# Narrow attention with outputs scaled by token and packed over two head groups, and layer-norm splits on GpSimd

## The reference

```
q, k, v = heads(h @ Wq), heads(h @ Wk), heads(h @ Wv)          # 16 heads of 16
a   = softmax(q k^T * 0.25)
x   = x + concat_heads(a v) @ W_proj + b_proj                   # 256 x 256
```

## Time and profile before

| | us |
|---|---|
| median of 3 runs (lowest, highest) | 4316.21 (4314.57, 4319.16) |
| profiled execution | 4317.04 |
| its span, first to last instruction | 4315.3 |
| mean granted clock of PE | 0.962 |
| PE, DVE, ACT, POOL busy | 3929.6 (91%), 3012.2 (70%), 2075.9 (48%), 1368.1 (32%) |

### The profile page before, as it was taken

One profiled execution on the slowest core, in us unless ns is written; L12 is line 12 of the kernel. 1 busy time (PEld: TensorE's weight loads), 2 busy tenths in 40 slices (PEclk: granted clock), 3 DMA queues, 4 the chain that ended last, 5 costly groups with the idle time before them and its releaser, 6 DMA issues.

```text
span 4315.3 us, 54472 instructions
## 1 busy us (share of the span) xinstructions
PE 3929.6 (91%) x19916; PEld 2380.8 (55%) x19916; DVE 3012.2 (70%) x4405; ACT 2075.9 (48%) x3756; POOL 1368.1 (32%) x664
## 2 busy tenths in 40 slices
PE   7999989799998888999899968988999999998989
PEld 5343346633334665555555546666555555546778
DVE  5888856788885676777777845445677777774465
ACT  2556655365665533444344436643444444445641
POOL 1100011200001035666566544421444444451120
PEclk7999989999999999999999989998999999998999
DMA  4233240313324133332233223323232333214320
GB/s 132 35 62 47 46 75 22 60 32 50 44 46 76 38 80 74 65 65 56 53 69 69 62 63 82 82 59 78 57 71 64 70 69 69 62 36 115 85 57 20
DMA packets 151979, 269.21 MB, mean 62 GB/s; under 512 B 34090, under 2 KB 67812, under 8 KB 150688
## 3 DMA queue, kind: packets, MB, share of 16 engines
q1 hardware_dynamic: 151712, 265.72, 29.2%
HBM read 105.01 MB, written 29.64 MB: 31 GB/s over the span
## 4 chain that ended last, share of the span: by engine, by line
PE 68%; DVE 16%; issue 4%; SPq 4%; ACT 4%; POOL 2%; DMA 2%; DVEq 0%; POOLq 0%; ACTq 0%
PE PS L1017 30%; PE PS L1196 13%; PE PS L1237 5%; PE PS L1089 4%; PE PS L1093 4%; DVE t L1764 3%; PE PS L1325 3%; PE PS L1247 3%; SPq L2177 2%; DVE t L1758 2%; SPq L2194 1%; DVE PS L1832 1%; DMA t<-t 1%; PE PS L1120 1%; PE PS L1206 1%
## 5 line engine op out<-in xcount | busy, mean ns | idle before, releaser
L1017 PE MATMUL PS<-t 128*128 128x512 f32 (+4 forms) x7896 | 1957.7, 379 | 127.3 <-DVE t L1673 16.5
L1470 ACT ACTIVATE t<-PS 128x512 f32<-128x512 f32 (+2 forms) x1600 | 1165.8, 750 | 989.2 <-PE PS L1017 982.9
L1017 PEld LDWEIGHTS PS<-t 128*128 128x128 f32 (+2 forms) x7896 | 1233.7, 184 | 637.1 <-issue 234.4
L1196 PE MATMUL PS<-t 128*32 128x512 f32 (+2 forms) x4352 | 808.3, 608 | 0.0
L1758 DVE TENSOR_REDUCE t<-PS 128x1 fp32r<-128x1024 f32 x512 | 618.4, 1218 | 232.2 <-PE PS L1089 231.3
L1764 DVE TENSOR_REDUCE t<-PS 128x1 f32<-128x512 f32 x1024 | 647.0, 682 | 65.1 <-PE PS L1093 62.3
L2038 POOL TENSOR_TENSOR t<-t 128x1024 f32<-128x1024 f32 x256 | 620.2, 2423 | 126.8 <-ACT t L1470 101.8
L1089 PE MATMUL PS<-t 128*128 128x512 f32 x1024 | 339.0, 414 | 70.0 <-DVE t L1758 35.6
L1093 PE MATMUL PS<-t 96*128 96x512 bf16 x1024 | 363.5, 392 | 37.6 <-DVE t L1764 21.3
L2034 POOL TENSOR_TENSOR t<-t 128x1024 f32<-128x1024 f32 x64 | 153.8, 2404 | 691.6 <-PE PS L1206 532.9
L1975 POOL TENSOR_TENSOR t<-t 128x2048 f32<-128x2048 f32 x24 | 111.1, 4628 | 819.2 <-DMA t<-in_rows 546.7
(11 more groups left out here) (131 smaller groups left out, 3713.6 us busy)
## 6 DMA issues: line engine op xcount, KB each, us to landing
t<-t SPq DMA_DIRECT2D x640, 128.0 KB, 2.5
t<-scr_n SPq DMA_DIRECT2D x288, 128.0 KB, 6.3
t<-t SPq DMA_DIRECT2D x128, 256.0 KB, 3.8
scr_n<-t SPq DMA_DIRECT2D x72, 256.0 KB, 2.5
t<-t SPq DMA_DIRECT2D x256, 64.0 KB, 2.0
t<-in_L_Wg SPq DMA_DIRECT2D x16, 768.0 KB, 4.6
t<-in_L_W SPq DMA_DIRECT2D x36, 256.0 KB, 3.3
t<-in_L_Wo SPq DMA_DIRECT2D x64, 128.0 KB, 2.4
```

The costliest lines, as they stand in the source:

```text
L1017: ins = e.matmul(out, l, r, start=i == 0, stop=i == len(terms) - 1, tile_position=tp)
L1196: ins = e.matmul(banks[S.ot][wd * j:wd * j + wd, :], u.v[j][kt], P[0:S.pr, j, :], start=kt == 0, stop=kt == S.nkt - 1, tile_position=(0, w ...
L1470: e.activation(dst, src, ACT.Exp, scale=S.L.scale).then_inc(*expd.inc((S.i, i)))
```

## The change

Three edits, in narrow attention and in the layer norms of blocks 0 and 1.

- **Scaling by token.** `sums16` becomes `scale16`: after the same four transposes, DVE takes the reciprocals and at once multiplies the 16 outputs of each head, read from PSUM, by the token's reciprocal, into columns 64 * `ends` of a tile `OT` (`ends` = `g % 2`). `spread16` and the old `norm` are gone.
- **Packing.** Two head groups (units n - 2 and n) fill the 128 columns of an `OT`. Only units with `ends` have a `turn16` (four PE transposes of `OT`, one ACT copy to `ON`) and the two `proj` steps. The projection weights are no longer padded: `S.W` holds 2 slices of 128 rows instead of 4.
- **Splits on GpSimd.** For 8 of the 24 parts (`on_pool`: in blocks 0 and 1 the parts (0,1), (1,0), (1,1) and (2,0), where the pair is sublayer and batch half) the two instructions of `ln_split` are issued on POOL.

The load of an unused constant (`sel`) is dropped, and SBUF pads keep the layout's size. The core of the diff:

```diff
@@ -671,7 +672,9 @@
                 plan.put(now, 0, [("av", S, an, akt)])
                 if akt == S.nkt - 1:
                     plan.put(now + 2e-4, 0, [("fin", S, an)])
-                    todo = [("sums16", S, an), ("spread16", S, an), ("norm", S, an), ("proj", S, an, 0), ("proj", S, an, 1)]
+                    todo = [("scale16", S, an)]
+                    if S.units[an].ends:
+                        todo += [("turn16", S, an), ("proj", S, an, 0), ("proj", S, an, 1)]
                     for at, step in zip(tail, todo):
                         plan.put(now + at, 0, [step])
 
...
@@ -544,7 +544,8 @@
                     u.st = [[[(buf[0:97, 1, j, 128 * kt:128 * kt + 128], buf[0:97, 0, j, q0:q0 + 512])]
                              for kt in range(8)] for j in range(4)]
                     u.v = [[S.VS[b][:, kt, h, :] for kt in range(8)] for h in u.heads]
-                u.wo = S.WO[g % 4]
+                u.wo = S.W[:, g % 4 // 2, :]
+                u.ends = g % 2
             else:
                 pi = u.pi
                 g = u.g = pi // 2
...
@@ -1214,13 +1217,14 @@
                 for q in range(4):
                     ins = e.transpose(o[:, 128 * q:128 * q + 128], S.OR[n % 2][:, 128 * q:128 * q + 128], ident[:, :])
                 ins.then_inc(*bank_full[k].inc(nth))
-            elif what == "norm" and a[0].L.style == 16:
+            elif what == "turn16":
                 S, n = a
-                w.wait_ge(spread, (S.i, n))
+                for m in (n - 2, n):
+                    k, nth = where["col", S.i, m]
+                    w.wait_ge(bank_free[k], nth)
                 o, k, nth = take(w, ring, ("norm", S.i, n))
                 for q in range(4):
-                    ins = e.transpose(o[:, 128 * q:128 * q + 128], S.RE[:, q, :, :].rearrange("p j d -> p (j d)"),
-                                      ident[:, :])
+                    ins = e.transpose(o[:, 128 * q:128 * q + 128], S.OT[n % 2][:, q, :], ident[:, :])
                 ins.then_inc(*bank_full[k].inc(nth))
             elif what == "proj":
                 S, n, i = a
@@ -1244,7 +1248,7 @@
                 o, k, nth = take(w, ring, ("proj", S.i, n, i))
                 for q in range(2):
                     at = 128 * (2 * i + q)
-                    ins = e.matmul(o[:, 256 * q:256 * q + 256], S.OR[n % 2][:, at:at + 128], u.wo[:, :],
+                    ins = e.matmul(o[:, 256 * q:256 * q + 256], S.ON[:, at:at + 128], u.wo[:, :],
                                    start=True, stop=True)
                 ins.then_inc(*bank_full[k].inc(nth))
             elif what == "kv16":
...
@@ -1335,6 +1339,9 @@
                 for r in rest:
                     w.wait_ge(r, a[0])
 
+    def on_pool(p):
+        return int(p.L.style == 16 and (p.s, p.b) in ((0, 1), (1, 0), (1, 1), (2, 0)))
+
     def proj_keys(S, n, i):
         return [("proj", S.i, n, i if S.L.style == 16 else 0)]
 
...
@@ -1402,7 +1409,8 @@
             elif what == "ln_turn":
                 p, q = a
                 if p.i or q:
-                    w.wait_ge(ln_split, (p.i, q - 1) if q else (p.i - 1, 3))
+                    was = p if q else line[p.i - 1]
+                    w.wait_ge(ln_split[on_pool(was)], (was.i, q - 1 if q else 3))
                 w.wait_ge(mod_made, (p.L.i, "all"))
                 o, k, nth = full(w, ("ln", p.i, q))
                 for c in range(2):
@@ -1472,9 +1480,8 @@
                 S, n = a
                 old = unit_before(S, n, 2)
                 if old:
-                    for key in proj_keys(old[0], old[1], 1):
-                        k, nth = where[key]
-                        w.wait_ge(bank_full[k], nth)
+                    k, nth = where[("col", old[0].i, old[1]) if S.L.style == 16 else proj_keys(old[0], old[1], 1)[0]]
+                    w.wait_ge(bank_full[k], nth)
                 w.wait_ge(weighed, (S.i, n, S.nkt - 1))
                 ot = banks[n % 2] if S.cross and S.L.style == 64 else banks[S.ot]
                 e.activation(S.OR[n % 2][:, :], ot, ACT.Copy).then_inc(*o_out.inc((S.i, n)))
@@ -1498,17 +1505,14 @@
                 o, k, nth = full(w, ("cturn", S.i, n))
                 e.activation(S.PT[n % 2][:, :, :], o[0:CT, :].rearrange("p (j q) -> p j q", j=2), ACT.Copy
                              ).then_inc(*bank_free[k].nth(nth))
-            elif what == "spread16":
+            elif what == "turn16":
                 S, n = a
-                old = unit_before(S, n, 1)
+                old = unit_before(S, n, 1 if n % 2 else 3)
                 if old:
-                    k, nth = where["norm", old[0].i, old[1]]
+                    k, nth = where["proj", old[0].i, old[1], 1]
                     w.wait_ge(bank_full[k], nth)
-                k, nth = where["col", S.i, n]
-                w.wait_ge(bank_free[k], nth)
-                r = S.R[n % 2][:, :, :].rearrange("p q (j o) -> p q j o", o=1)
-                e.activation(S.RE[:, :, :, :], r.broadcast_to([128, 4, S.nh, 128 // S.nh]), ACT.Copy
-                             ).then_inc(*spread.inc((S.i, n)))
+                o, k, nth = full(w, ("norm", S.i, n))
+                e.activation(S.ON[:, :], o, ACT.Copy).then_inc(*bank_free[k].nth(nth))
             elif what == "kv16":
                 S, = a
                 L = S.L
@@ -1649,7 +1653,7 @@
                 w.wait_ge(ln_recip, p.i)
                 e.tensor_scalar(XN[:, t % 4, :], X[:, 8 * p.b + t, :], ln_mv[:, t, 0:1], ln_sd[:, t:t + 1],
                                 ALU.subtract, ALU.mult).then_inc(*ln_normed.inc((p.i, t)))
-            elif what == "ln_split":
+            elif what == "ln_split" and not on_pool(a[0]):
                 p, q = a
                 k, nth = where["ln", p.i, q]
                 w.wait_ge(bank_free[k], nth)
...
@@ -1658,10 +1662,10 @@
                     k, nth = where[h_end(old[-1])]
                     w.wait_ge(bank_full[k], nth)
                 ts = slice(256 * q, 256 * q + 256)
-                e.tensor_copy(p.H[0][:, :, ts], HF[:, :, :]).then_inc(*ln_high.inc((p.i, q)))
-                w.wait_ge(ln_high, (p.i, q))
+                e.tensor_copy(p.H[0][:, :, ts], HF[:, :, :]).then_inc(*ln_high[on_pool(p)].inc((p.i, q)))
+                w.wait_ge(ln_high[on_pool(p)], (p.i, q))
                 e.tensor_tensor(p.H[1][:, :, ts], HF[:, :, :], f(p.H[0][:, :, ts]), ALU.subtract
-                                ).then_inc(*ln_split.inc((p.i, q)))
+                                ).then_inc(*ln_split[on_pool(p)].inc((p.i, q)))
             elif what == "w_split":
                 p, g, own = a
                 whi, wlo, stage = w_views(p)
@@ -1816,14 +1820,20 @@
                     w.wait_ge(vec_summed, (S.i, n, kt - 1))
                 e.tensor_tensor(S.AP_[:, :, :], S.AP_[:, :, :], S.P[p_slot(S, n, kt)[0]][:, :, :], ALU.add
                                 ).then_inc(*vec_summed.inc((S.i, n, kt)))
-            elif what == "sums16":
+            elif what == "scale16":
                 S, n = a
+                ends = S.units[n].ends
                 old = unit_before(S, n, 2)
-                if old:
-                    w.wait_ge(spread, (old[0].i, old[1]))
+                if old and not ends:
+                    k, nth = where["norm", old[0].i, old[1]]
+                    w.wait_ge(bank_full[k], nth)
                 o, k, nth = full(w, ("col", S.i, n))
-                e.reciprocal(S.R[n % 2][:, :, :], o.rearrange("p (q j d) -> p q j d", q=4, j=4)[:, :, :, 16]
-                             ).then_inc(*bank_free[k].nth(nth))
+                o = o.rearrange("p (q j d) -> p q j d", q=4, j=4)
+                e.reciprocal(S.R[n % 2][:, :, :], o[:, :, :, 16]).then_inc(*recip_made.inc((S.i, n)))
+                w.wait_ge(recip_made, (S.i, n))
+                r = S.R[n % 2][:, :, :].rearrange("p q (j o) -> p q j o", o=1).broadcast_to([128, 4, 4, 16])
+                to = S.OT[n % 2][:, :, 64 * ends:64 * ends + 64].rearrange("p q (j d) -> p q j d", j=4)
+                e.tensor_tensor(to, o[:, :, :, 0:16], r, ALU.mult).then_inc(*bank_free[k].nth(nth))
             elif what == "norm" and a[0].L.style == 64:
                 S, n, h = a
                 hs = slice(256 * h, 256 * h + 256)
...
@@ -1834,18 +1844,14 @@
                 ins = e.tensor_tensor(S.OR[n % 2][:, hs], S.OR[n % 2][:, hs], o[:, hs], ALU.mult)
                 if h:
                     ins.then_inc(*bank_free[k].nth(nth))
-            elif what == "norm":
-                S, n = a
-                w.wait_ge(o_out, (S.i, n))
-                o, k, nth = full(w, ("norm", S.i, n))
-                e.tensor_tensor(S.OR[n % 2][:, :], S.OR[n % 2][:, :], o[:, 0:512], ALU.mult).then_inc(*bank_free[k].nth(nth))
             elif what == "proj":
                 S, n, i = a
                 p = S.units[n].part
                 T = 8 * p.b + S.units[n].q0 // 128 + 2 * i
                 w.wait_ge(biased, p.i)
-                if n >= 2:
```

(34 more changed lines are left out.)

26 lines of the change are left out of this document (9 added, 17 removed).

## The result

The changed kernel took 4259.77 us (median of 4 runs, 4254.4 to 4263.81), the kernel before 4315.39 beside it: ratio 0.9863, 95% interval 0.9849 to 0.9878, 55.6 us faster. The forecast was 73 us. Its profiled execution took 4261.02 us, its span is 4258.8, the mean granted clock 0.958.

A forecast was written before the change was run, and what follows sets the result against it. PE was taken to bound self attention with DVE next, and cross attention to shift between mixed, DMA, DVE and PE. Self 21.5 plus cross 15 us, over two blocks 73 us, took 4316.2 to 4243 us; range 4205 to 4285.

The forecast's parts named there:

- Pace and bound: Self attention: 28.4 us a unit, PE fullest, DVE next with 3.4 us slack; cross: mixed, DMA, near DVE's limit, then PE.
- 2.0 between DVE's 1.64 and PE's 2.36: Self attention: packing gains 2.0 us in each of eight units without `ends`, 16 us a stage.
- Splits in self attention: Self attention: moving the splits off DVE gains 5 us a stage, of which the subtraction holds 0.9% of the chain.
- the pair 12, 13: Late cross attention: PE falls from 4.6 to 2.3 us a unit, ACT bounds at about 2.7, gaining 3.8 us.
- more than forecast: Cross attention, 590 to 607 us: PE idles less, clock returns, collision gone whole; toward 4188 us; chance 0.08.
- DMA: no gain: Cross pair 4, 5 gains 0, since the chain waits 5.86 us for maxima queued behind the head stacks.
- Collision: Cross attention: a DVE split copy took 4.63 us behind POOL's bias addition; avoiding it counted 3.5 of 4.2 us.
- The order for the old lengths: Attention units: due times suit old lengths, so gains overlap with waits; lower end of the gain, 4277 us; chance 0.12.
- GpSimd and DVE collide: Moved norm quarters: DVE waits out a 1.3 us POOL instruction in all 32, returning 42 us, 4285 us; chance 0.08.
- ACT's modulation waits on POOL: Layer norms with moved splits: sign that the forecast is wrong, tied to the rival of a slow POOL rounding copy.
- Slower: Cross-part norms: a slow POOL rounding copy, decisive from 6.5 us, holds ACT; 4341 us at 8 us; chance 0.08.

The follow-up runs named there:

- e1: The changed kernel with all layer-norm splits back on DVE, packing kept: 4266.52 us, ratio 0.9870 to the kernel before.
- e5: The changed kernel without packing, every unit turned and projected, products on 128 rows padded with zeros: 4296.79 us, ratio 0.9959 to the kernel before.
- e2: The kernel before with only the layer-norm splits of the eight parts moved to GpSimd: 4306.84 us, ratio 0.9965.
- e4: The changed kernel without packing, every unit turned and projected with products of 64 rows: 4348.87 us, ratio 1.008 to the kernel before.
- e3: The changed kernel with later due times for PE's transposes and projections in all cross units: 4255.57 us, ratio 0.9852 to the kernel before.
- e7: The kernel before with the GpSimd bias addition issued in four pieces of 512 columns instead of one of 2048: 4299.38 us, ratio 0.9960.

## Why the prediction was right, and where it was off

- **Pace and bound: right.** PE leads in self attention, DVE is next, cross attention changes on its way. In self attention two intervals behind light units, of before and of the changed kernel, show the price:

```profile
L1825 DVE RECIPROCAL t<-PS x3: 247/247/247, 276.4 to 330.0; 128x16 f32<-128x16 f32 x3
```

```profile
L1832 DVE RECIPROCAL t<-PS x3: 247/247/247, 271.4 to 320.1; 128x16 f32<-128x16 f32 x3
```

  53.6 us fall to 48.7, 2.45 a light unit. I took 2.0 between DVE's 1.64 and PE's 2.36. In these two, PE's whole price comes back: DVE's slack of 3.4 us a unit was enough. Not so in all: in e1, which moves no split, a light unit gains 1.5 to 3.0 us, 2.2 in the mean of block 0 and 2.3 of block 1.
- **Splits in self attention: over-sized.** 5 us forecast, 1 to 3 measured. The chain's 0.9% for L1663 was read as time that would go; when the split goes, the chain can run through the next instruction. That the self stages come out near 21.5 (19.0 to 22.1 in four stages) is part luck: packing was sized too low at 16.5 (18.7 in e1's block 1), the splits too high.
- **Cross attention: the pair 12, 13 failed.** I put ACT next, at 2.7 us a unit as a sum of busy times with small waits. Its 2.2 us of work came from the mean of ten unlike instructions, 0.73; an exponential there takes 1.02, so that the three are 2.6. Even so the measured 3.9 and 3.6 us are not that sum: exponentials, copy out, transposes and the next scores form a loop in which each waits for the one before, since the transposes stand ahead of the next scores in PE's order. A sum of busy times is no bound where the order closes a loop.
- **Cross attention: the clock.** The forecast put the clock at nothing, and only the rival *more than forecast* moved it, upward, with less idling in 590 to 607 us. In units 0 to 2 it stayed (0.72 before, 0.73 after), and behind them it fell. From the windows, (0.90 - 0.81) * 33.8 + (0.95 - 0.87) * 29.2 + (1.00 - 0.91) * 19.6 = 7.1 us of PE at full clock were not granted in block 0, an upper estimate of what it cost. The packed kernels have the lower clock in this stage (0.81 to 0.88), e5 without packing has not (0.96 and 0.94). That it comes of PE doing less and waiting more between is argued, not shown. In units 11 to 15 two executions of the changed kernel part the two causes. In the second profile no low stretch falls there in block 0:

```profile
648.30:666.50 18.20, 15.14 (x97) 8.38 (x95) 6.24 (x17) 10.34 (x14) 7.12 (x4) 1.00 0.03 8
```

  The pair takes 3.9 and 3.6 us in both, but the last unit 4.2 us at a clock of 1.00 against 5.6 with a low stretch in it. So of the 3.8 us forecast for this pair the loop left about 2 (20.2 against 18.2 us), and the clock took 1.4 of these in the first profile. The MLP stages too lose 1 to 4 us in some executions with the clock; the program there is the same, and e2, which packs nothing, loses 2 to 4 there as well (135.8 and 128.6 us).
- **DMA: no gain, as forecast, but a loss in block 1.** I forecast 0 for units 2 to 7. Block 0 gained 1.0 us. Block 1 lost 4.3 (38.2 against 33.9) in the first profile and 1.1 (35.0) in the second. In the first, PE's wait for that DMA there is

```profile
PEld PS L1020 <- DMA t<-t: 5.3, 1, 5.3
```

  My argument had nothing that could make this stretch longer; why it did, and why by different amounts in two executions, stays open. The stretch varies in every kernel: 31.1 to 34.8 us in the profiles without packing (e4 left out), 31.6 to 39.0 in those with it.
- **Collision: right in place, near in size.** Of 4.2 us in a cross stage I counted 3.5; e2 gains 4.2 in those units. It moved to the q copy as named, 2.5 to 3.4 us in one copy of each narrow stage. What I left out is that the long instruction itself could be cut, and that this is worth at least as much as the move.
- **Rivals.** *The order for the old lengths* is in part what happened, in cross attention only; changing due times brought at most 4 us. *GpSimd and DVE collide* happened in small: 11 of the 96 `ln_norm` steps of the narrow blocks meet a moved split on POOL and take 0.64 to 1.32 us instead of 0.40, 5 us of DVE in all, where the rival had 42. That ACT's modulation waits on POOL, which I named as a sign of being wrong, was seen, with 3.4 us in block 0 (5.8 us for DVE's split before). *Slower* needed a copy of 6.5 us; it takes 0.62, nearer to the estimate from the Trainium skill's one-input rule (GPSIMD Engine Reference, Engine selection), 0.5, than to my 0.9.

The sum by the first profile: self 21.8 + 19.0, cross 12.4 + 8.2, MLP products -1.4 - 3.0, block 2 and 3 -0.5 by difference: 56.5 us between the spans. So the forecast of 73 us was 9 to 17 us too high, most of it in cross attention and the MLP stages behind it. How much of that is the clock and how much the loop stays open outside units 11 to 15: e3 removed the loop and kept the low clock (0.83 in both cross stages), and no run here sets the clock alone.

## What to carry to other kernels

When work is taken out of the leading engine in every second unit, look at what its order puts behind the freed place: if a step waits for another engine's copy there, the unit falls to the length of that loop, not to the next engine's load. One long GpSimd instruction from SBUF to SBUF held each VectorE copy or subtraction from SBUF to SBUF that met it here until its end; try cutting it before moving work between the two engines. And before a product of 128 rows padded with zeros is replaced by one of 64 rows, look at the granted clock.

## What the runs showed of the hardware

- Products of 64 rows: with PE fully busy (38.5 of 38.5 us) the granted clock stayed at 0.50 over 109 us, and the kernel that differs from it mainly in padding to 128 rows with zeros ran at 1.00 there. The two are some 50 us of 4300 apart (4348.87 and 4296.79). At a clock of 1.00 a product of 64 rows is no faster than one of 128: 0.376 and 0.379 us in self attention of block 0 (medians of e4 and e5).
- A rounding copy of 128x512 fp32 on GpSimd takes 0.62 us, a subtraction of that size 1.27; on VectorE 0.42 and 0.69.
- A VectorE copy of 0.42 us that starts behind a 4.51 us GpSimd addition takes 4.63 us (kernel before), a subtraction of 0.69 us 4.88 (e1). With the addition cut in four, the copies in that place take at most 1.40 (e7). A VectorE step that reads PSUM and SBUF took its 0.69 us beside such an addition.
